# Who adds, scales and sums the step sizes of a state space mixer, and when: POOL and VectorE at the head of a Trainium2 kernel

## The reference

```python
dt_raw = proj[..., 2 * H * P + 2 * H * N:]
dt = jax.nn.softplus(dt_raw + dt_bias)
xc = jax.nn.silu(_causal_conv(x_ssm, conv_w_x))
...
A = -jnp.exp(A_log)
decay = jnp.exp(dt * A)
dtx = dt[..., None] * xc
```

## Time and profile before

| | |
|---|---|
| median of three executions | 717.81 us (717.26 to 717.88) |
| the profiled execution | 717.6 us |
| its span in the trace | 715.9 us |
| PE busy | 650.2 us, 91% |
| DVE busy | 538.2 us, 75% |
| ACT busy | 454.1 us, 63% |
| POOL busy | 478.0 us, 67% |

### The profile page before, as it was taken

The page is one execution under the profiler, slowest core; times in us unless marked ns, Lnnn a source line. Parts: engine busy times, 40 slices in busy tenths (PEclk is TensorE's granted clock), DMA queues, the critical chain, the costliest instruction groups (busy, mean ns, idle before and its releaser), DMA issues.

```text
span 715.9 us, 11648 instructions
## 1 busy us (share of the span) xinstructions
PE 650.2 (91%) x3364; PEld 513.1 (72%) x3364; DVE 538.2 (75%) x856; ACT 454.1 (63%) x743; POOL 478.0 (67%) x452
## 2 busy tenths in 40 slices
PE   6589999999999999999999999999978998799920
PEld 3477878878878878878878878788847766477710
DVE  4879999999999999999999999589415583123336
ACT  3376887887887887887887887774224553233321
POOL 4066779878888887897898795859063668653034
PEclk9899999999999999999999999999999999899965
DMA  4312121121121121121121130320638614444124
GB/s 149 125 45 69 63 77 61 50 96 59 45 103 59 45 103 59 45 103 59 45 103 59 45 103 0 119 95 15 167 92 231 262 38 118 116 137 111 53 74 132
DMA packets 26258, 63.11 MB, mean 88 GB/s; under 512 B 5222, under 2 KB 18918, under 8 KB 23494
## 3 DMA queue, kind: packets, MB, share of 16 engines
q1 hardware_dynamic: 23062, 54.09, 22.3%
q0 software_dynamic: 3168, 8.67, 4.7%
HBM read 53.56 MB, written 9.20 MB: 88 GB/s over the span
## 4 chain that ended last, share of the span: by engine, by line
PE 67%; DVE 13%; issue 6%; ACT 5%; DMA 2%; POOL 2%; another core or an unknown queue 2%; SPq 0%; DVEq 0%; ACTq 0%; POOLq 0%
PE ps L715 26%; DVE conv L1488 7%; PE ps L743 7%; PE ps L729 5%; PE ps L987 5%; PE ps L1027 4%; PE ps L660 3%; PE ps L678 3%; ACT decay L1165 3%; DVE decay L1472 2%; PE ps L730 2%; PE ps L700 2%; PE ps L1005 1%; PE ps L875 1%
## 5 line engine op out<-in xcount | busy, mean ns | idle before, releaser
L1488 DVE SCALAR_TENSOR_TENSOR conv<-ps,w_raw,conv 128x506 f32<-128x506 f32 (+3 forms) x352 | 320.8, 935 | 19.3 <-ACT conv L1159 14.6
L715 PE MATMUL ps<-x_hi,w_hi 128*128 128x512 f32 x384 | 160.0, 417 | 9.7 <-DVE conv L1488 8.6
L1159 ACT ACTIVATE conv<-ps,w_raw 128x512 f32<-128x512 f32 x160 | 108.2, 686 | 73.6 <-PE ps L715 73.4
L715 PE MATMUL ps<-x_hi,w_lo 128*128 128x512 f32 x384 | 152.1, 396 | 0.0
L715 PE MATMUL ps<-x_lo,w_hi 128*128 128x512 f32 x384 | 151.3, 394 | 0.0
L427 POOL TENSOR_TENSOR decay<-cum_b,cum_tok 128x512 f32<-128x512 f32 (+1 forms) x128 | 103.5, 831 | 23.7 <-DVE cum_tok L1433 23.7
L715 PEld LDWEIGHTS ps<-x_hi,w_hi 128*128 128x128 f32 x384 | 73.1, 190 | 28.3 <-DVE conv L1488 10.2
L433 POOL TENSOR_TENSOR decay<-decay,mask 128x512 f32<-128x512 f32 x64 | 82.5, 1289 | 5.0
L715 PEld LDWEIGHTS ps<-x_hi,w_lo 128*128 128x128 f32 x384 | 72.8, 190 | 17.0
L715 PEld LDWEIGHTS ps<-x_lo,w_hi 128*128 128x128 f32 x384 | 73.3, 191 | 12.9
L729 PE MATMUL ps<-conv 128*128 128x256 f32 x256 | 79.5, 392 | 1.8 <-DVE decay L1472 0.3
(11 more groups left out here) (236 smaller groups left out, 1064.9 us busy)
## 6 DMA issues: line engine op xcount, KB each, us to landing
cum_b<-cum_scratch SPq DMA_DIRECT2D x16, 1024.0 KB, 4.7
w_raw<-in_winT SPq DMA_DIRECT2D x16, 778.0 KB, 4.4
y_all<-in_wgu SPq DMA_DIRECT2D x4, 1408.0 KB, 19.1
ys_scratch<-y_blk SPq DMA_DIRECT2D x31, 128.0 KB
late<-in_wdn SPq DMA_DIRECT2D x2, 1408.0 KB
x_scratch<-conv SPq DMA_DIRECT2D x19, 128.0 KB, 3.3
late<-in_woutT SPq DMA_DIRECT2D x1, 2048.0 KB, 8.3
res_scratch<-conv SPq DMA_DIRECT2D x11, 128.0 KB
```

The lines of the kernel that those rows point to most:

```text
L715: mm = pe.matmul(ps[:, j % 4, :], wp[:, par, w], xp[:, kk, t], start=(i == 0), stop=(i == 5))
L1159: act.activation(conv[:, par, tile, hf * 512:(hf + 1) * 512], ps[:, j % 4, :], ACT.Copy, scale=w_raw[:, par, tap:tap + 1]).then_inc(S["a_c ...
L1488: dve.scalar_tensor_tensor(out=o[:, :, s:], in0=u[:, :, 0:T - s], scalar=w_raw[:, par, c:c + 1], in1=o[:, :, s:], op0=ALU.mult, op1=ALU.ad ...
```

## The change

The add and the multiplication of the step sizes move from DVE to POOL, behind `split(1, 1)`. What is left of `sum_dt` on DVE, the four scans, moves from in front of the taps of unit 1 to in front of those of unit 2.

```diff
@@ gpsimd @@
             pool.wait_ge(S["w_split"], 2)
             split(1, 1)
+            pool.wait_ge(S["a_dt"], 5)
+            pool.tensor_tensor(dt_l, dt_l, dt_ch, ALU.add).then_inc(S["d_dt"], 1)
+            pool.wait_ge(S["d_dt"], 1)
+            pool.tensor_scalar(dt_da, dt_l, head_c[:, 2:3], -1.0, ALU.mult, ALU.mult).then_inc(S["d_dt"], 1)
             pool.wait_ge(S["st_cum"], 16)
             pool.wait_ge(S["d_dtT"], 1)
             log_decay(0, 0, 0)
@@ vector @@
             def sum_dt():
 
-                made = [0]
-
-                def link(ins):
-
-                    made[0] += 1
-                    ins.then_inc(S["d_dt"], 1)
-                    dve.wait_ge(S["d_dt"], made[0])
-                dve.wait_ge(S["a_dt"], 5)
-                link(dve.tensor_tensor(dt_l, dt_l, dt_ch, ALU.add))
-                link(dve.tensor_scalar(dt_da, dt_l, head_c[:, 2:3], -1.0, ALU.mult, ALU.mult))
+                dve.wait_ge(S["d_dt"], 2)
                 for b in range(NB):
                     t = slice(b * T, (b + 1) * T)
                     ins = dve.tensor_tensor_scan(dt_cum[:, t], one[:, :].broadcast_to([H, T]), dt_da[:, t], 0.0, ALU.mult, ALU.add)
-                link(ins)
+                ins.then_inc(S["d_dt"], 1)
+                dve.wait_ge(S["d_dt"], 3)
@@ vector, step @@
                 if isinstance(n, int) and n == 0:
-                    between[1, 0] = [sum_dt]
+                    between[2, 0] = [sum_dt]
```

## The result

The changed kernel takes 715.79 us (median of 17, 714.87 to 717.89), the kernel before 718.78 us on the same chip (17, 716.98 to 720.06). The two medians lie 3.0 us apart. The ratio over all executions is 0.9965, with a 95% interval of 0.9955 to 0.9975: by it the change is 2.5 us faster, 1.8 to 3.2, and this is the figure that I use. The forecast was 718.4, no change.

The account below looks back on a forecast made before the run. The prediction took DVE's queue to set the start of step 1. Its terms, -0.05 us at unit 3 and +0.65 for PE's second gap, gave +0.6 on 717.81, so 718.4 us, range 715.8 to 719.6.

Parts of the forecast that it names:

- What bounds the head: Before step 1: DVE's queue sets its start; 4.5 us of step size work stand in front of unit 1.
- Unit 1 goes first: On DVE: unit 1 starts at 20.43 instead of 24.30 us, and PE restarts at 23.87 instead of 27.73.
- The add: On POOL: the add of the step sizes starts at 19.91 us and takes 2.39 us, by interpolation.
- I take 4.28, as the row is the same instruction with two operations: On POOL: the scaling of 1024 elements takes 4.28 us, extrapolated from a 256-element row.
- Nearly all comes back as the wait for POOL: On DVE before the scans: a wait of 2.33 us for POOL, leaving net -0.05 us at unit 3.
- rival 1: POOL's scaling takes 2.4 us or less, so unit 3 starts 1.97 to 2.4 us earlier; 715.4 to 716.8 us, chance 0.17.
- PE's second gap: Before half 8: PE idles 4.1 to 6.0 us, then runs at a lower clock; cost 0 to 1.0, taken as 0.65 us.
- the forecast's own case: POOL's scaling takes 4.28 us and PE's second gap costs 0.65 us, giving 718.4 us; chance 0.45.
- Rival 2: Start of step 1: denser half tiles before it keep PE's clock up, giving back 1.6 us; 716.8 us, chance 0.10.
- What the later sums cost: Behind the scans: SP's loads go out 4.9 us later, but POOL wants the first only at 42.02 us; no cost.

Follow-up runs that it names:

- second pair of traces: The kernel before and the changed kernel, both unaltered, timed and traced again; the gain at the load of pair 3's weights is 3.31 us.
- pool_dear: The changed kernel with POOL's scaling made four times over, so that it lasts 4.72 us; ratio to the kernel before 1.0037.
- before_warm: The kernel before with 4 extra, unused matmuls on PE behind the transposes of the sums; ratio to the kernel before 0.9996.
- copy_first: The changed kernel with ACT's log behind the copy of half 3 and the scans before unit 3; pair 3's weights load at 53.13 us from ACT's first copy.
- forms: The changed kernel with nine extra TENSOR_SCALAR instructions on POOL behind its scaling, some beside DVE's scans; the scans took 3.63 us.
- forms_apart: The changed kernel with the same nine extra POOL instructions as forms, now behind DVE's scans; the scans took 2.42 us.

## Why the prediction was wrong, point by point

- **What bounds the head** was right: DVE's queue from unit 1 to take_dt, with PE's long gap and the late copy of half 7 as echoes.
- **Unit 1 goes first**: 6.50 us after ACT's first copy by the forecast (20.43 - 13.93), 6.46 measured. The add: 2.39, measured 2.36.
- **"I take 4.28, as the row is the same instruction with two operations"**: this is the step that failed. It took 1.11 us. The row of line 555 subtracts and multiplies, the new instruction multiplies twice, and the first operation made the row dear. I had put the doubt on the wrong thing, the operands from memory. The Trainium skill's sentence that one input is roughly at line rate (GPSIMD Engine Reference, 4.1 Engine selection), which I had set aside for that row, fits the multiplications: the estimate of 1.2 us that I had worked out by that page is close to the 1.11 measured, 0.83 ns for each further element. It does not fit the subtraction (3.3 ns).
- **"Nearly all comes back as the wait for POOL"** followed from that price. At 1.11 DVE's own queue decides; rival 1 gave 2.4 us for it, and 2.56 are measured at take_dt (2.05 in the second pair of traces, where DVE waited for half 9).
- **PE's second gap** was not 4.1 to 6.0 us but 1.99, and in the first trace it cost nothing, as unit 4 did not wait. Its size in the forecast's own case was too small, 1.7 instead of 0.65 (pool_dear). I had taken 4.62 us as the most that two half tiles cost behind a long gap, but in the rows I took it from the last matmuls were already back at the full clock (0.39 us each from 31.66 on, where the ones before took 0.63); wholly at the low clock two half tiles took 5.29.
- **Rival 2**, the clock at the head of step 1, came too. I priced it at 1.6 us and it is 1.3 (before_warm). I treated it as apart from rival 1; the two came together in both traces of the change. The head gained 3.9 us in the first pair, the sum of both (2.56 and 1.30), and 3.3 in the second. That my time for either rival alone lies near the measured one is therefore luck: neither described what happened, and the late stages took a part back.
- **What the later sums cost**: nothing, as forecast. POOL's idle time before its first decay ends with DVE, even in copy_first, where they are later still.
- The whole kernel gained 2.5 us, less than the 3.9 of the head's trace. A low-clock stretch between lines 359 and 363 takes 0.8 in the first pair. The second pair, on another chip, kept 3.3 up to the first output's store, counted from ACT's first copy (683.47 - 14.28 = 669.19, against 680.26 - 14.40 = 665.86). The 2.5 is also what DVE's queue alone would give, if the clock's 1.3 were lost on the way to the end as in before_warm. Which of these makes the ratio is open.

## What to carry to other kernels

Price an instruction that moves to POOL by a row with the same operations, not only of the same kind: here subtract-multiply cost over three times as much as multiply-multiply at 1024 elements. If the whole change hangs on such a price, ask at which value it turns and weigh the chances by how sure the row is. Here 4.33 us was the value at which unit 3 breaks even; with the second gap's 1.7 us behind it the change loses from a lower price on, an estimated 3.2 us by pool_dear's trace (4.72 - 1.55), if the clock is as low behind the shorter gap.

Work given to a slower engine gains only if the freed engine has something to put in front of its return. Each half of this change alone gained nothing that the runs show.

When a long gap of PE is cut into pieces, look at which half tiles run at the lower clock behind each piece, and whether somebody waits for them. In copy_first the gap stood in front of the last ones, and DVE waited 1.22 us for the transposes behind them. Follow a gain at the head to the end of the program before counting it: before_warm's 1.3 us were not seen there.

## What was not expected of the hardware

- POOL and DVE slow each other beside DVE's scans: the four scans took 3.63 us instead of 2.42, POOL's multiplication of 128x256 took 0.72 instead of 0.48, and with both operands from memory 1.24 instead of 0.55 (forms against forms_apart). The Trainium skill names such contention for DVE instructions with two inputs in SBUF (GPSIMD Engine Reference, 1. Specifications), which the scans have. In the changed kernel POOL is through 0.9 us before the scans, and they took 2.41.
- The chips differ in the late stages. From the expert weights' load (line 359) to the first output's store (line 378) the kernel before took 158.8 us on one (698.29 - 539.48) and 143.5 on another (683.47 - 539.95), while the mixer took the same time (525.55 and 525.67 from ACT's first copy to line 359). About 7 of these 15 us lie between lines 359 and 363 (13.83 and 6.87 us). Just before line 359, PE waits 3.60 us on the first chip, up to 539.39, and no such wait is in the other trace. What makes the chips differ is open.
